# Second attention: scores computed twice, the second time with keys on partitions

## The reference

```
q, k, v = (qkv[:, :, i].transpose(0, 2, 1, 3) for i in range(3))
attn = jax.nn.softmax(jnp.einsum('bhqd,bhkd->bhqk', q, k) * hd ** (-0.5), axis=-1)
o = jnp.einsum('bhqk,bhkd->bhqd', attn, v).transpose(0, 2, 1, 3).reshape(B, T, D)
```

## Time and profile before

| | us |
|---|---|
| median of the runs | 4012.0 |
| the profiled execution, device time | 4011.16 |
| its span, first to last instruction | 4009.4 |
| from the first score of the second attention to the first instruction of the next stage | 1079 |
| mean time of one tile in it | 2.08 |

### The profile page before, as it was taken

How to read it: one execution, slowest core, us unless ns; L and a number is a source line. 1 busy time by engine, 2 the same in 40 slices (tenths; PEclk the granted TensorE clock), 3 DMA queues, 4 the chain that set the end, 5 groups by cost and what they waited for, 6 DMA issues and landing times. The chain is left out here.

```text
span 4009.4 us, 70221 instructions
## 1 busy us (share of the span) xinstructions
PE 3775.5 (94%) x26756; PEld 2543.0 (63%) x26756; DVE 2721.6 (68%) x4863; ACT 2687.9 (67%) x4667; POOL 1035.5 (26%) x1544
## 2 busy tenths in 40 slices
PE   8997999999999986999999959799999999995999
PEld 7885666666666664778888835466666666662555
DVE  4335888888888876444421148688888888885987
ACT  2226888888888854222222238688888888884998
POOL 0004555555555465000000037100000000002554
PEclk9998999999999998999999979899999999997999
DMA  5446233333333088244531038733332333313221
GB/s 189 184 164 152 62 67 62 67 62 67 62 67 62 14 285 272 100 137 158 176 114 53 32 131 303 205 62 67 62 67 62 67 61 67 62 30 127 77 80 51
DMA packets 307567, 419.53 MB, mean 105 GB/s; under 512 B 89449, under 2 KB 165741, under 8 KB 307227
## 3 DMA queue, kind: packets, MB, share of 16 engines
q1 hardware_dynamic: 307232, 415.03, 36.8%
HBM read 257.34 MB, written 157.32 MB: 103 GB/s over the span
## 5 line engine op out<-in xcount | busy, mean ns | idle before, releaser
L555 ACT ACTIVATE Sn<-Sn,mn 128x1024 f32<-128x1024 f32 x1024 | 1174.8, 1147 | 30.4 <-DVE mn L583 19.0
L521 PEld LDWEIGHTS pt<-ident,Sn 128*128 128x128 f32 x8192 | 881.2, 141 | 420.8 <-issue 413.5
L521 PE MATMUL pt<-ident,Sn 128*128 128x128 f32 x8192 | 1123.4, 280 | 1.0 <-DVE PT L547 0.4
L545 ACT ACTIVATE PT<-pt 128x512 f32<-128x512 f32 x1280 | 738.2, 597 | 236.0 <-PE pt L521 235.9
L489 PE MATMUL sp<-KS,QS 97*128 97x512 f32 (+1 forms) x2048 | 733.6, 440 | 45.3 <-DMA KS<-s_khi 23.6
L583 DVE CUSTOM_DVE_ANT_0 Sn<-sp,biastile 128x1024 f32<-128x1024 f32 x512 | 624.4, 1220 | 145.1 <-PE sp L489 113.5
L585 DVE TENSOR_SCALAR_CACHE_REDUCE Sn<-sp 128x1024 f32<-128x1024 f32 x512 | 624.3, 1220 | 137.3 <-PE sp L489 137.3
L628 POOL TENSOR_SCALAR biastile<-dist,ascale 128x1024 f32<-128x1024 f32 x512 | 576.3, 1126 | 497.0 <-DVE mn L583 483.9
L510 PE MATMUL po<-PT,Vp 128*32 128x256 f32 x8192 | 651.4, 391 | 0.0
L547 DVE COPY PT<-pt 128x512 f32<-128x512 f32 x768 | 531.2, 692 | 118.5 <-PE pt L521 118.3
L1077 ACT ACTIVATE gf<-pf,b1T 128x512 f32<-128x512 f32 x128 | 88.3, 690 | 535.4 <-PE pf L1022 530.5
(11 more groups left out here) (237 smaller groups left out, 4985.8 us busy)
## 6 DMA issues: line engine op xcount, KB each, us to landing
QS<-s_qhi SPq DMA_DIRECT2D x128, 256.0 KB, 5.0
KS<-s_khi SPq DMA_DIRECT2D x128, 256.0 KB, 7.2
KS<-s_klo SPq DMA_DIRECT2D x64, 256.0 KB, 6.1
QS<-s_qlo SPq DMA_DIRECT2D x64, 256.0 KB, 6.9
Vp<-s_v SPq DMA_DIRECT2D x64, 256.0 KB, 7.8
s_o<-og SPq DMA_DIRECT2D x32, 512.0 KB, 8.7
xA<-in_x SPq DMA_DIRECT2D x8, 1024.0 KB, 5.7
s_qhi<-qstage SPq DMA_DIRECT2D x32, 256.0 KB, 2.0
```

Of the source, the lines that this page charges most:

```text
L521: op = nc.tensor.transpose(ps[:, i, :], sn[:, (g * HALF + i) * P:(g * HALF + i + 1) * P], K.ident[:])
L545: nc.scalar.activation(dst, src, ACT.Copy).then_inc(*s_cp_act.up())
L555: nc.scalar.activation(sn[:], sn[:], ACT.Exp, scale=-1.0, bias=mn[n % 3][:, t:t + 1], accum_out=sums[n % 5][:, t:t + 1]).then_inc(*s_exp.up())
```

## The change

`stage_attention(K, 1)` becomes a function of its own, `stage_attention1`. The first attention stays as it was.

- The scores are computed twice: once as before (queries on partitions), from which VectorE takes only the minimum, without a copy; and a second time with keys on partitions (`score_turned`), from which ScalarE takes the exponential directly into `pT`. The transposes of the exponentials and their copies are gone.
- The minimum enters the second product as two more rows: 98 rows in place of 96. GpSimd splits it in a high and a low half (`minima_halves`), eight fp32 matmuls per head with two columns of weights and the 128x128 identity as the moving side turn it into rows (`minima_to_rows`), and ScalarE copies these under q (`rows_to_queries`).
- The row sums come from matmuls with ones (`total`), after GpSimd has added the exponentials of two key blocks (`add_pair`), both in fp32.
- The order on TensorE goes by windows of 4 tiles (half a head): first all 16 score products, then, in every even window, `minima_to_rows`, or in every odd one `turn_output` (four transposes), then `times_v` four times and `total` twice.
- The PSUM buffers: 2 of 1024 columns for the first scores; 2 of 512 columns (`pst_r`) that the second scores, the minima's rows and the turned output share; one of 256 columns each for the output and the sums.

The core of the new function:

```
        def score_turned(u, g):
            n, kb = divmod(u, LT)
            p, j = divmod(n, PAIR)
            pe.wait_ge(s_row, n + 1)
            pe.wait_ge(s_neg, 1)
            ps = pst_r.take(pe, ("st", u, g), (s_exp, 2 * u + g + 1))
            nc.tensor.matmul(ps[:], ks_l.at[p][0][0:ROWS + 2, j, kb * P:(kb + 1) * P], qs_l.at[p][0][0:ROWS + 2, j, g * BLK:(g + 1) * BLK],
                             start=True, stop=True).then_inc(*s_st.up())

        def minima_to_rows(n):
            ps = pst_r.take(pe, ("row", n), (s_row, n + 1))
            pe.wait_ge(s_mm, n + 1)
            for t in range(LT):
                r0 = ROW_AT[t * P // BLK]
                op = nc.tensor.matmul(ps[r0:r0 + 2, t * P % BLK:t * P % BLK + P], mm[n % 2][:, t, :].bitcast(F32), K.ident[:],
                                      start=True, stop=True)
            op.then_inc(*s_mrow.up())

        def total(m):
            n, k = divmod(m, LT // 2)
            pe.wait_ge(s_two, m + 1)
            if k == 0:
                pe.wait_ge(s_ov, n)
            for g in range(4):
                op = nc.tensor.matmul(pz[g * HD:(g + 1) * HD, :], K.ones[:, 0:HD], two[m % 3][:, g * QW:(g + 1) * QW],
                                      start=k == 0, stop=k == LT // 2 - 1)
            op.then_inc(*s_sum.up())

        def tensor_program():
            for w in range(NW + TAIL):
                for i in range(4):
                    if 0 <= w - 3 < NW:
                        score_turned(4 * (w - 3) + i, 0)
                    if w < NW:
                        score(4 * w + i, 0)
                    if w < NW and i == 3:
                        score(4 * w + i, 1)
                    if 0 <= w - 3 < NW:
                        score_turned(4 * (w - 3) + i, 1)
                    if w < NW and i < 3:
                        score(4 * w + i, 1)
                n, odd = divmod(w - 2, 2)
                if not odd and 0 <= n < N_HEADS:
                    minima_to_rows(n)
                n, odd = divmod(w - 7, 2)
                if not odd and 0 <= n < N_HEADS:
                    turn_output(n)
                if 0 <= w - 4 < NW:
                    for i in range(4):
                        times_v(4 * (w - 4) + i)
                    for i in range(2):
                        total(2 * (w - 4) + i)
...
            nc.scalar.activation(pT[n % 2][:, kb, g * BLK:(g + 1) * BLK], pst_r.at["st", u, g][:], ACT.Exp, scale=-1.0).then_inc(*s_exp.up())
...
            nc.vector.tensor_reduce(mn[n % 2][:, t:t + 1], ps_r.at[u][:], AX.X, ALU.min).then_inc(*s_min.up())
...
        def vector_program():
            for w in range(NW + TAIL):
                if w < NW:
                    minimum(4 * w)
                n, odd = divmod(w - 6, 2)
                if not odd and 0 <= n < N_HEADS:
                    take_output(n)
                if w < NW:
                    for i in range(1, 4):
                        minimum(4 * w + i)
                n, odd = divmod(w - 7, 2)
                if not odd and 0 <= n < N_HEADS:
                    output(n)
...
            nc.gpsimd.tensor_tensor(two[m % 3][:], pT[n % 2][:, 2 * k, :], pT[n % 2][:, 2 * k + 1, :], ALU.add).then_inc(*s_two.up())
```

166 lines of the change are left out of this document (165 added, 1 removed).

## The result

| | before | after |
|---|---|---|
| median of the runs, us | 4013.67 (4 runs) | 4089.38 (4 runs) |
| profiled execution: span, us | 4009.4 | 4086.8 |
| first score to next stage, us | 1079 | 1155 |
| a head of the second attention, us | 16.65 | 17.64 |

The ratio to the kernel before is 1.0196, 95% interval 1.0184 to 1.0209: the kernel became 76 us slower. The forecast was 4095, so the total and its direction came out. Several of its terms did not, and they cancelled in part.

The account below looks back on a forecast made before the run. TensorE's stream was taken as the bound before; after, waits in its queue raise a head from 16.65 to 17.86 us: +77 over 64 heads, +7 for the ends, +84 on 4011.2 gives 4095 us, range 3990 to 4165.

Parts of the forecast that it names:

- TensorE's stream was the bound before, and its work falls: Second attention: TensorE's instructions set the time before the change; their sum falls from 16.65 to 15.5 us a head.
- The loop through 2 buffers: Score part: second scores wait for exps to free PSUM buffers, 1.18 us per two exps against 0.93 of products.
- The even window behind minimum 1: Even windows: output copies delay VectorE's second minimum, first scores wait for it, and the score products take 5.11 us.
- The minima's products, 1.75 us: TensorE, even windows: eight fp32 products turning minima into rows, 0.218 us each with nothing beside them, 1.75 us a head.
- The ends: Stage's start and finish outside the 64 heads: some 20 us, less work absent there, against 13 before: +7.
- The sum: Second attention: odd window 8.10 and even window 9.76 us, 17.86 a head against 16.65, +77 us over 64 heads.
- What the ring costs: 150 us, without it the change would win: Score parts: waits on the second scores' 2 buffers and minimum 1 cost 2.4 us a head, 150 us in all.
- The signs named: Expected trace: TensorE idle 100 us or more, exps spaced 0.49 and 0.69 us, even windows 1.6 us longer than odd.
- TensorE as the bound: Rival: TensorE's stream still sets the pace and the 2 buffers don't hold it up; 3946 us, chance 0.13.
- Half of the wait: Rival: hand-overs overlap more, so half the score part's wait goes; 4020 us, from 3990 to 4060, chance 0.12.
- Minima's weight loads: Rival: weight loads of the minima's products show, 1.75 us more a head, +110, 4205 us; chance 0.07.
- GpSimd: Rival: GpSimd's adds take over 4 us and bind; at 4.3, 18.7 us a head, 4149 us; chance 0.04.

Follow-up runs that it names:

- the last of these runs: Changed kernel without GpSimd's adds and the totals, with 3 buffers for the second scores and the output copies ahead of the first minimum: 3891.53 us.
- The version that won: Changed kernel with output copies first, alternating minima products, and one total a window through a third add on GpSimd, VectorE's output behind the fourth minimum: 3988.54 us.
- the kernel with three edits: Changed kernel with output copies first, minima products alternating between quarters, and one total a window, VectorE adding GpSimd's two sums: 4004.65 us.

## Why the prediction was right, and where it wasn't

- **TensorE's stream was the bound before, and its work falls.** Right as far as it was tested: the run without sums took 0.43 us a block off the windows, the price read from the stream of v. That the kernel before was bound by it rests on the earlier trace rows alone; no run changed that kernel.
- **The loop through 2 buffers.** Right as a mechanism: a longer exp lengthened it, a third buffer ended its waits. Its size was 0.31 too small in the odd window (5.03, not 4.72). The term was the hand-over towards ScalarE, taken at 0.04 from the one towards VectorE. Measured, an exp ends at 3114.00, its successor's product starts at 3114.06 and with 0.50 ends at 3114.56, and the next exp starts at 3114.65: 0.09 on that side, 1.24 for the pair (other pairs 1.25 to 1.27) against 1.18.
- **The even window behind minimum 1.** Right: 5.30 against 5.24, and moving the copies brought 12 us.
- **The minima's products, 1.75 us.** Wrong in size. Minima and v's part took 3.99 against the forecast's 4.52 (0.88 + 3.11 against 1.81 + 2.71). Only 1.26 us of it is the minima's (3.99 less the odd window's 2.73). The failed step is "consecutive ones use the same quarter of the partitions, so nothing runs beside them": the second quarter's ran beside the first's, and v's beside both. The price inside one quarter held, 0.109 an instruction. Of the bounds the lower one, 0.87, was slightly nearer than the 1.75 that was taken, and the upper one, 3.5, was far off.
- **The ends.** +7 was forecast. 1155 - 64 x 17.64 = 26 against 13 before is +13. The three windows without second scores took 18.9 us, where VectorE's pace gave 13.7: a tile took 1.27 there, not 1.14, and behind the last one the first head's minima products and their hand-over took 3.95, which no term of the forecast names.
- **The sum.** 17.64 a head against 17.86: +0.25 in the odd window and -0.47 in the even one. The error in the total, 6 us, is smaller than either term (16 and 30 us over 64 heads), so that it is so small is luck. A right total is no proof of its terms.
- **"What the ring costs: 150 us, without it the change would win".** Not borne out. Ring and copies gave 83 us of the 150, and with the 115 us of the sums back on top of 3891.53 that is 4007, level with the kernel before. (That is an estimate; no run has the sums and 3 buffers.) What failed is the assumption that nothing stands behind the ring: with a third buffer the first scores waited for minima, 118.5 us of 900 in the last of these runs. The version that won got there by fewer totals and by the order, not by the ring.
- **The signs named.** Even windows were longer than odd ones by 0.94 us, not 1.6, and exps stood 0.49 and 0.75 us apart in turn, not 0.49 and 0.69. These are the two mis-sized terms again. TensorE's idle time of 100 us or more appears only in the weight loads: the matmul rows show 24 us of 1000 idle.
- **The rivals.** TensorE as the bound is out by the longer exp. Half of the wait is out: it gave 4020, at most 4060. Minima's weight loads, out: their products stand 0.109 apart in one quarter. GpSimd, out by the run without sums.
- **The Trainium skill's rule on weight loads** ("TensorE: Matmul & The Clock Gate", Part 3) was weighed and set aside on the trace. That held: F32R products stayed at 0.23 to 0.24 us.

## What to carry to other kernels

Average busy time says little once an in-order queue passes through a small ring: write down one round of the ring (consumer, hand-over, fresh product, hand-over) and compare it with the producer's work in that round, both here within 0.1 us of what was measured. Before moving work away from behind a step, ask which waits it was covering: the interleaving that removed short waits for exps laid open one of 1.6 us and one of 0.8 us a head. A buffer added to one ring hands the time to the next limit, so read the waits again before claiming the sum.

## What the runs showed of the hardware that was not expected

- Products that write different quarters of the PSUM partitions start out of program order: v's first two start 0.10 to 0.32 us before the last three of the minima's 16 that stand ahead of them. The Trainium skill ("TensorE: Matmul & The Clock Gate", Part 3, What overlaps and what doesn't) has matmuls start in strict program order. This trace shows otherwise for column tiles of different quarters.
- An fp32 addition of 128x1024 with both inputs in SBUF took VectorE 2154 to 2840 ns in the kernel with three edits, each time while GpSimd was at the like addition, and GpSimd stayed at 2377. Two of them, from the timeline of the kernel with three edits, each below the GpSimd add that it overlaps:

```profile
3107.95 2.38 POOL L874 TENSOR_TENSOR two<-PT 128x1024 f32<-128x1024 f32 x1 [0.99 <-ACT PT L784]
...
3109.23 2.18 DVE L841 TENSOR_TENSOR four<-two 128x1024 f32<-128x1024 f32 x1
```

```profile
3100.02 2.38 POOL L874 TENSOR_TENSOR two<-PT 128x1024 f32<-128x1024 f32 x1 [2.50 <-ACT PT L784]
...
3100.66 2.83 DVE L841 TENSOR_TENSOR four<-two 128x1024 f32<-128x1024 f32 x1
```

The first overlaps for 1.10 us, to 3110.33, and takes 2.18; the second for 1.74, to 3102.40, and takes 2.83. Both are the overlap and 1.1 us more, and so are all 110 of them between 2600 and 3500 us (1.08 to 1.09 more). So VectorE made next to no progress while GpSimd's addition ran. The kernel before has a like operation of VectorE, an fp32 subtraction of 128x1024 with both inputs in SBUF, in another stage. Alone it takes 1.22 to 1.23 us. Beside a GpSimd addition that started first it takes the overlap and 1.1 us, too, and where VectorE started first it is GpSimd that is held, 2.15 us in place of 1.28 (timeline of the kernel before):

```profile
1468.87 1.28 POOL L879 TENSOR_TENSOR xbC<-xC,b2b 128x512 f32<-128x512 f32 x1
1469.51 1.72 DVE L705 TENSOR_TENSOR w1l<-wraw,w1h 128x1024 fp32r<-128x1024 f32 x1
...
1479.04 1.19 DVE L705 TENSOR_TENSOR w2l<-wraw,w2h 128x1024 fp32r<-128x1024 f32 x1
1479.24 2.15 POOL L879 TENSOR_TENSOR xbC<-xC,b2b 128x512 f32<-128x512 f32 x1 [0.80 <-DMA s_x<-xbC]
```

In these traces, then, the one of the two that started first ran on at its own pace and the other stood still. The minima, which read PSUM, were not held: their mean was 1220 ns in the changed kernel, with GpSimd busy for 56% of the stage.
